# Narrowing tokens with a second tensor, and a GpSimd share of two or three tiles, in the up stage of a decoder layer

## The reference, cut to what matters

```python
def _L0_ffn_ref(x, clip_x, clip_down, w_gate, w_up, w_down):
    ...
    xq = _act_fake_quant(x, clip_x[0])          # x: the layer norm's output, (4, 1024, 256)
    gate = jnp.einsum('bsh,ih->bsi', xq, _weight_fake_quant(w_gate))
    up = jnp.einsum('bsh,ih->bsi', xq, _weight_fake_quant(w_up))      # i = 704
    h = _act_fake_quant(jax.nn.silu(gate) * up, clip_down[0])
    return jnp.einsum('bsi,hi->bsh', h, _weight_fake_quant(w_down))
...
x = x + _L0_ffn_ref(_layernorm(x, axis=-1), ...)
```

## Time and profile before

| | us |
|---|---|
| median of three runs | 702.86 |
| the profiled execution, its own time | 700.23 |
| its span, first to last instruction | 698.3 |
| TensorE busy | 609.3 (87%) |
| VectorE busy | 519.2 (74%) |
| ScalarE busy | 407.6 (58%) |
| GpSimd busy | 164.8 (24%) |
| mean granted TensorE clock | 0.961 of full speed |

### The profile page before, as it was taken

One profiled execution on the slowest core, in us unless ns is written; L12 is line 12 of the kernel. 1 busy time (PEld: TensorE's weight loads), 2 busy tenths in 40 slices (PEclk: granted clock), 3 DMA queues, 4 the chain that ended last, 5 costly groups with the idle time before them and its releaser, 6 DMA issues.

```text
span 698.3 us, 19983 instructions
## 1 busy us (share of the span) xinstructions
PE 609.3 (87%) x8015; PEld 394.0 (56%) x8020; DVE 519.2 (74%) x985; ACT 407.6 (58%) x602; POOL 164.8 (24%) x213
## 2 busy tenths in 40 slices
PE   2799999999999999999999999999989943887395
PEld 2556575766765766576757656576547532333173
DVE  6698877878788576757866866686697566699777
ACT  3345666675675448556555476543554714999682
POOL 2013332421343302320431033220120001455200
PEclk9899999999999999999999999999999966999789
DMA  7643133562344344256324363433384320000024
GB/s 255 184 155 127 48 120 104 143 151 72 104 143 104 108 112 105 71 140 158 114 48 146 76 148 101 112 107 94 85 224 101 74 53 0 0 1 1 0 91 152
DMA packets 58554, 72.17 MB, mean 103 GB/s; under 512 B 23979, under 2 KB 35423, under 8 KB 58463
## 3 DMA queue, kind: packets, MB, share of 16 engines
q1 hardware_dynamic: 54783, 68.92, 35.7%
q10 hardware_dynamic: 3680, 1.97, 1.1%
HBM read 17.74 MB, written 4.72 MB: 32 GB/s over the span
## 4 chain that ended last, share of the span: by engine, by line
PE 52%; DVE 19%; SPq 10%; DMA 7%; issue 6%; ACT 4%; POOL 1%; DVEq 0%; ACTq 0%; POOLq 0%
PE banks L483 34%; PE banks L663 5%; SPq L416 5%; DVE mneg L1097 4%; PE banks L674 3%; PE banks L583 3%; SPq L434 2%; DVE tops L1281 2%; PE banks L527 2%; DMA oc<-sums 2%; PE banks L728 1%; DVE big L1275 1%; DVE parts L1263 1%; DVE mneg L1101 1%; DMA oTs<-oe 1%
## 5 line engine op out<-in xcount | busy, mean ns | idle before, releaser
L483 PE MATMUL banks<-big 96*128 96x77 bf16 (+3 forms) x1344 | 158.9, 239 | 9.8 <-DVE mneg L1101 3.1
L1097 DVE TENSOR_REDUCE mneg<-banks 128x4 f32<-128x640 f32 (+3 forms) x128 | 127.0, 1019 | 40.0 <-PE banks L592 39.5
L899 ACT ACTIVATE big<-banks 128x1024 f32<-128x1024 f32 (+1 forms) x128 | 122.2, 974 | 58.1 <-PE banks L483 45.0
L1378 POOL TENSOR_SCALAR_AFFINE_SELECT big<-big 128x512 f32<-128x512 f32 x128 | 85.0, 664 | 287.8 <-ACT big L899 286.9
L483 PEld LDWEIGHTS banks<-big 99*128 99x128 bf16 (+2 forms) x1344 | 103.1, 102 | 77.1 <-issue 31.9
L483 PE MATMUL banks<-xnT,weights 128*128 128x512 f32 x192 | 91.7, 606 | 0.2 <-DVE mneg L1097 0.2
L903 ACT ACTIVATE big<-banks 77x1024 f32<-77x1024 f32 x64 | 63.6, 1020 | 46.9 <-PE banks L483 30.9
L583 PE MATMUL banks<-big 96*32 96x160 bf16 (+3 forms) x1792 | 71.2, 258 | 0.6 <-DVE mneg L1097 0.2
L663 PE MATMUL banks<-big 128*17 128x256 f32 (+1 forms) x1152 | 70.8, 346 | 0.3 <-ACT oe L912 0.2
L1101 DVE TENSOR_REDUCE mneg<-banks 128x8 f32<-128x616 f32 x64 | 49.3, 791 | 16.5 <-PE banks L483 16.2
L728 PE MATMUL banks<-oe,weights 128*128 128x512 bf16 x187 | 46.8, 394 | 10.8 <-DVE big L1275 4.4
(11 more groups left out here) (152 smaller groups left out, 1111.4 us busy)
## 6 DMA issues: line engine op xcount, KB each, us to landing
big<-parts SPq DMA_DIRECT2D x285, 128.0 KB, 2.5
oc<-sums SPq DMA_DIRECT2D x16, 512.0 KB, 4.8
oTs<-oe SPq DMA_DIRECT2D x64, 64.0 KB, 2.4
out_dram<-oTs SPq DMA_DIRECT2D x16, 256.0 KB, 2.3
xs<-in_x_dram SPq DMA_DIRECT2D x3, 1024.0 KB, 5.7
big<-oe SPq DMA_DIRECT2D x32, 64.0 KB, 2.3
oTx<-oe SPq DMA_DIRECT2D x32, 64.0 KB, 2.3
xs<-in_x_dram SPq DMA_DIRECT2D x2, 512.0 KB, 6.4
```

What stands on the lines that cost most here:

```text
L483: return e.matmul(to[0:w], k[:, 0:w], q, start=start, stop=stop, skip_group_check=True)
L899: e.activation(pt[u].rearrange("p (i n) -> p i n", i=4)[:, :, 0:n], pair(p).rearrange("p j (s n) -> p (j s) n", s=2)[:, :, 0:n], ACT.Exp, ...
L1097: e.tensor_reduce(M.rearrange("p (h c) -> p h c", h=4)[:, :, c], pair(p).rearrange("p j (s n) -> p (j s) n", s=2)[:, :, 0:160 + 32 * (c % 4)],
L1378: e.affine_select(out=P[:, :, 0:128], in_=P[:, :, 0:128], compare_op=ALU.is_ge, fill=0.0, base=0, pattern=[[0, 4], [1, 128]], channel_mult ...
```

## The change

Two things change, both in the up stage. Narrowing becomes `scalar_tensor_tensor`: the mean stays a per-partition scalar, and the inverse deviation, one number per partition, is now a second tensor that repeats it over 256 columns. The share of GpSimd becomes tiles 1, 3 and 5 in even blocks and tiles 1 and 5 in odd ones; tile 3 of blocks 1, 3, 5 and 7 goes to VectorE, and ScalarE doesn't scale it. GpSimd then has 20 products and VectorE 28, where each had 24. The rest of the diff counts the semaphores by a table in place of a formula.

```diff
+        def pool_tiles(blk):
+            return (1, 5) if blk % 2 else (1, 3, 5)
+
+        turn_of, turns = {}, [0, 0]
+        for blk in range(8):
+            for t in range(FT):
+                on_pool = t in pool_tiles(blk)
+                turn_of[blk, t] = turns[on_pool]
+                turns[on_pool] += 1
+        POOL_ALL = turns[1]
...
-                return (f_u, 3 * s[1] + (s[2] + 1) // 2) if s[2] % 2 else (f_hd, 3 * s[1] + s[2] // 2 + 1)
+                return (f_u, turn_of[s[1:]] + 1) if s[2] in pool_tiles(s[1]) else (f_hd, turn_of[s[1:]] + 1)
...
-                        hid_wait(e, n - 4)
+                        e.wait_ge(*hid_done(*divmod(n - 4, FT)))
...
-                elif k == "hid" and s[2] % 2:
+                elif k == "hid" and s[2] in pool_tiles(s[1]):
...
+        def hid_done(blk, t):
+            return (f_hp if t in pool_tiles(blk) else f_hd), turn_of[blk, t] + 1
...
-                    e.tensor_scalar(x8[:, at:at + 256], xs[:, t0, :], mv[:, t0, 0:1], rstd[:, t0:t0 + 1], ALU.subtract,
-                                    ALU.mult).then_inc(f_x8, 1)
-                elif k == "hid" and s[2] % 2 == 0:
+                    e.scalar_tensor_tensor(x8[:, at:at + 256], xs[:, t0, :], mv[:, t0, 0:1],
+                                           rstd[:, t0:t0 + 1].to_broadcast([128, D]), ALU.subtract, ALU.mult
+                                           ).then_inc(f_x8, 1)
+                elif k == "hid" and s[2] not in pool_tiles(s[1]):
...
-                    e.wait_ge(f_hd, 3 * blk + t0 // 2 + 1)
-                    e.wait_ge(f_hp, 3 * blk + t0 // 2 + 1)
+                    e.wait_ge(*hid_done(blk, t0))
+                    e.wait_ge(*hid_done(blk, t0 + 1))
```

More of the change, by code:

```diff
@@ L977, in run_scalar @@
                     e.activation(sgb[:, i:i + 512], bank(p), ACT.Silu, scale=winv[:, t0:t0 + 1]).then_inc(f_silu, 1)
-                elif k == "hid" and s[2] % 2:
+                elif k == "hid" and s[2] in pool_tiles(s[1]):
                     _, blk, t0 = s
-                    m = 3 * blk + t0 // 2
+                    m = turn_of[blk, t0]
                     p = f_bank["up", blk, t0][0]
@@ L990, in run_scalar @@
                     e.wait_ge(f_sc, 12)
-                    e.wait_ge(f_hp, 24)
+                    e.wait_ge(f_hp, POOL_ALL)
                     if blk > 1:
@@ L1402, in run_gpsimd @@
                 k = s[0]
-                if k == "hid" and s[2] % 2:
+                if k == "hid" and s[2] in pool_tiles(s[1]):
                     _, blk, t0 = s
-                    n, m = n_up(blk, t0), 3 * blk + t0 // 2
+                    n, m = n_up(blk, t0), turn_of[blk, t0]
                     i = (n % 4) * 512
```

## The result

The kernel after takes 705.68 us, the median of 13 runs (703.6 to 708.37). The kernel before, in 13 runs beside it, takes 700.96 (698.97 to 704.75). The ratio is 1.0059, with a 95% interval of 1.0040 to 1.0078: slower by 0.6%, 4.1 us of 701. (The two medians lie 4.7 us apart; the ratio is estimated from all the runs.) The span of the profiled execution grew from 698.3 to 702.2 us.

The account below looks back on a forecast made before the run. VectorE was taken to set the up stage's pace, ScalarE and TensorE held to it through PSUM banks. 0.32 + 0.13 + 0.21 + 0.17 + 0.20 + 1.15 + 0.66 = +2.84 us on 702.86 gave 705.7 us, range 701.3 to 708.5.

Parts of the forecast that it names:

- The narrowing's price: Each narrowing in the up stage, in its new form, takes 0.48 us against 0.401, 0.08 more each.
- rival 3: Slow second stream: each narrowing costs 0.34 us more at the upper bound, +7.3 in all, 710.1 us; chance 0.05.
- The hold: First pairs of narrowings: GpSimd's product still holds the new form; held pairs end 0.59 us after GpSimd, not 0.39.
- rival 2: The new narrowing is not held by GpSimd, so the hold goes: -0.7, 702.1 us; chance 0.13.
- 3-4: Block 3's t=2 product to block 4's: block 4's `up` waits for the moved product's PSUM bank, +1.15 us.
- Start: Before the cast that ScalarE waits for at 587.87: four dearer narrowings, 4 x 0.08 = +0.32 us.
- P: Block 1's first product to its t=2 product: the first pair's second narrowing is held as now, +0.13 us.
- 4-5: Block 4's t=2 product to block 5's: a shorter wait eats the narrowings' growth before GpSimd's end, +0.17 us.
- 1-2: Block 1's t=2 product to block 2's: the shrinking hold almost pays for the moved product, +0.20 us.
- 2-3: Block 2's t=2 product to block 3's: a shorter wait eats the narrowings' growth before GpSimd's end, +0.21 us.
- Blocks 5 to 7: End of the up stage: block 5's growth of 0.8 us vanishes in VectorE's waits; block 7's moved product adds +0.66.
- Rival 1: The hold on the five first pairs doesn't shrink, so everything adds: +4.6, 707.4 us; chance 0.22.

Follow-up runs that it names:

- the run without reads: The kernel after with GpSimd's product replaced by a constant fill that writes SBUF and reads nothing; its stage takes 70.33 us.
- block 3 kept: The kernel after, but block 3 keeps three tiles on GpSimd; 704.47 against 701.64 us for the kernel before, ratio 1.0031.
- The kernel that keeps block 5: The kernel after, but block 5 keeps three tiles on GpSimd; 708.32 us in its only run, 56.71 us from block 1's first product to the last top's end.
- the one that keeps block 7: The kernel after, but block 7 keeps three tiles on GpSimd; 704.44 against 701.64 us for the kernel before, ratio 1.0029.

## Why the prediction came out as it did, step by step

The forecast was 705.7 us and the median is 705.68, but part of that is luck: it was built on 702.86 for the kernel before, which in the longer series has 700.96. What counts is the difference, +2.8 forecast against +4.1 (2.8 to 5.5) in the whole and +3.66 in the stage. Most of my weight lay on no change beyond 0.5%, and the ratio of 1.0059 is just over that line.

- *What bounds.* Right: VectorE stays full, and ScalarE's relief buys nothing.
- *The narrowing's price.* Right: 0.472 against 0.48. A second tensor that repeats one word costs no more than the plain one that the sum was made from, so rival 3, the slow second stream, is out. "Vector Engine (DVE) Microarchitecture Reference", in "Measured stream behaviour on trn2" of the Trainium skill, has 1.73 ns a column for a source without adjacent pairs; my estimate from it was 0.65 us, and this trace shows that a repeated word is not such a case.
- *The hold.* Right: it stays, and rival 2 is out. "SBUF — State Buffer", in "Who interferes with whom" of the Trainium skill, has two SBUF inputs contend with a GpSimd instruction that reads, and not with one that only writes: the trace agrees for the new form (1.509 us beside the multiply, 0.480 at most beside the fill). My price for the rival was off: I said -0.7, and in the run without reads the stage is at +0.2. I had left the banks out of it: the end costs +1.30 there where I had +0.66, and 3-4 takes 7.88 where I had 7.63.
- *Start* (+0.32, measured 16.45 - 16.17 = +0.28 to block 1's first product), *P* (+0.13, +0.14), *4-5* (+0.17, +0.19): right. *1-2* (+0.20, +0.10): right in mechanism, the moved product of block 1 is paid by a shorter hold (pair of 1.04 us); GpSimd began 5.89 us after the t=2 product and not 5.99.
- *3-4* (+1.15, measured +1.27): right in place, mechanism and nearly in size: with block 3 kept 1.06 of it goes, and 0.21 stays for the new form.
- *2-3* (+0.21, measured +0.39): undersized. GpSimd's product starts 6.08 us after the t=2 product at 613.86 and ends at 621.20, not 5.89 after it. The kernel with the narrowing alone keeps 7.76, so this comes from block 1's moved product, one block later. The held pairs fit this: about 1.0 us in block 3 and 0.84 in block 5, where I had 0.6 to 0.8. The trace of the kernel after shows why GpSimd is 0.2 late, by the same step that failed in block 6, only smaller. Block 2's first product comes 5.02 us behind block 1's t=2 product, 4.22 before; the `up` of block 2, tile 3 needs its bank, so that tile's Silu waits 0.53 us (613.01 in the rows); ScalarE's copy of the turned tokens is late by it, and TensorE waits for the copy before it starts block 3 (616.01). This chain was read from one trace and not tested by a run:

```profile
613.01 0.69 ACT L988 ACTIVATE xnT<-banks,winv 128x512 f32<-128x512 f32 x1 [0.53 <-PE banks L728]
...
616.01 2.75 PE L728 MATMUL banks<-oe,weights 128*128 128x512 bf16 x12 [0.32 <-ACT oe L977]
```

- *Blocks 5 to 7* (+0.66, measured +1.29): the step that failed. I wrote that the growth of block 5's moved product "vanishes" in VectorE's waits. VectorE did have the idle time, but the product delays block 6's first one, whose bank the `up` of tile 3 needs; TensorE, ScalarE, and with them block 7, come later. The kernel that keeps block 5 gives 0.62 back, and the one that keeps block 7 0.64, the +0.66 that I had. I had looked the banks up for tile 3's own readers only and not for the products behind it.
- *The down stage* was to shift as a whole; it took 0.67 more in the profiled execution, with 0.47 us of idle time before an addition and a longer wait for an output DMA. Two profiles of one program differ by 0.86 us there, so nothing says that it belongs to the change.
- *Rival 1*, holds that don't shrink, is not what happened, if narrowly: they shrank from 4.8 to 4.1 us, where about 4.3 would have spoken for it. All of the shrinking is in block 2's pair (from 1.0 to 0.2 us), and the idle time before block 7's first product stayed (1.02 us). Its total of +4.6 was near for another reason.

## What to carry to other kernels

When two engines are both nearly full, the wait that one of them suffers is worth little more than the other's slack: when the holds on VectorE fell from 4.8 to 2.1 us, the stage gained 0.8. When a work item changes engines, look up every consumer of its output buffer and of the buffers behind it in the queue; here one instruction with a step of 0.66 us cost between 0.2 and 1.04 us. The table of banks says where it delays others; how much of that counts, only the engines' waits in that block say (blocks 1 and 5 have the same entries). A short instruction that a neighbour holds up is moved in time before it is rewritten.

## What the runs showed of the hardware that I had not expected

- The two forms of narrowing differ in what holds them: against a GpSimd that only writes, `tensor_scalar` went to 1.118 us and `scalar_tensor_tensor` stayed at 0.480 or less.
- TensorE's granted clock fell to 0.50 for about 3 us in the middle of a busy stage, after a wait of 1.44 us, in one profile of a kernel and not in the other, taken on another chip, with the same wait. The kernel after waited 1.58 us at the same place and kept 1.00.
